# Two attention layers with two feed-forward layers: rows normalised by VectorE, and scores on four 64 by 64 tiles of TensorE with a softmax by even and odd heads

## What is computed

```
x = x + attention0(layernorm(x), ctx)      # 16 heads of 64, q = x@Wq, k = ctx@Wk, v = ctx@Wv
x = x + ffn0(layernorm(x))                 # silu(x@Wg) * (x@Wu), hidden 768, then @Wd
x = x + attention1(layernorm(x), ctx)      # a second set of weights
x = x + ffn1(layernorm(x))                 # rows and weights rounded to int8, product, scaled back

attention: scores = q @ k.T * 64**-0.5     # per head: 256 x 77
           attn   = softmax(scores)        # over the 77 keys
           out    = (attn @ v) @ Wo + bo
```

## Time and profile before

| | |
|---|---|
| median of 3 runs | 1615.76 us (1608.71 to 1623.88) |
| the profiled execution, its span | 1612.4 us |
| PE matmuls busy | 1554.2 us (96%), 27282 matmuls |
| ScalarE busy | 1371.5 us (85%) |
| VectorE busy | 1364.5 us (85%) |
| GpSimd busy | 1273.3 us (79%) |
| granted TensorE clock over the span | 0.992 of 2.4 GHz |

### The profile page before, as it was taken

One profiled execution on the slowest core, in us unless ns is written; L12 is line 12 of the kernel. 1 busy time (PEld: TensorE's weight loads), 2 busy tenths in 40 slices (PEclk: granted clock), 3 DMA queues, 4 the chain that ended last, 5 costly groups with the idle time before them and its releaser, 6 DMA issues.

```text
span 1612.4 us, 74691 instructions
## 1 busy us (share of the span) xinstructions
PE 1554.2 (96%) x27282; PEld 1438.8 (89%) x27282; DVE 1364.5 (85%) x3522; ACT 1371.5 (85%) x5640; POOL 1273.3 (79%) x1893
## 2 busy tenths in 40 slices
PE   7989898999999999999999999999999999999996
PEld 4555578999999999999999999999999999999995
DVE  6767567888888888888888887888898988998886
ACT  6656588899899989998999988889999999999984
POOL 5100088899999898999998988788999999999984
PEclk9999999999999999999999999999999999999998
DMA  9997689887887777878778999899899899988996
GB/s 262 366 274 250 232 170 186 169 175 173 183 166 173 177 173 169 176 173 183 166 173 179 171 173 160 154 183 189 193 200 199 190 192 193 202 191 193 190 189 124
DMA packets 740024, 307.81 MB, mean 191 GB/s; under 512 B 629201, under 2 KB 725361, under 8 KB 737841
## 3 DMA queue, kind: packets, MB, share of 16 engines
q1 hardware_dynamic: 738049, 299.32, 85.0%
q0 software_dynamic: 1840, 6.82, 1.4%
HBM read 87.09 MB, written 65.54 MB: 95 GB/s over the span
## 4 chain that ended last, share of the span: by engine, by line
PE 33%; POOL 32%; issue 11%; DVE 6%; DMA 3%; ACT 2%; SPq 1%; POOLq 0%; ACTq 0%; DVEq 0%
PE psum L328 25%; POOL pr L1660 10%; POOL p L1665 8%; POOL p L1673 6%; PE psum L1225 4%; POOL rs L388 3%; POOL hT_l L1651 3%; PE psum L326 2%; DMA pT<-p 2%; DVE oT_l L357 1%; PE psum L319 1%; DVE x L1640 1%; POOL y L1702 1%; ACT ex L1371 1%; DMA x2T<-x 1%
## 5 line engine op out<-in xcount | busy, mean ns | idle before, releaser
L1371 ACT ACTIVATE ex<-psum,nmax 128x77 f32<-128x77 f32 x2048 | 638.3, 336 | 43.2 <-DVE nmax L1499 35.9
L1665 POOL TENSOR_TENSOR p<-pr,p 128x308 f16<-128x308 f32 x512 | 414.2, 809 | 39.9 <-ACT p L343 1.8
L1371 ACT ACTIVATION_READ_ACCUMULATOR ex<-psum,nmax 128x1 f32 x2048 | 444.7, 217 | 0.0
L1660 POOL TENSOR_TENSOR pr<-ex,rden 128x308 f32<-128x308 f32 x512 | 375.0, 732 | 55.2 <-DVE rden L1504 54.5
L328 PE MATMUL psum<-xT,wq_h 128*64 128x256 f16 x4064 | 349.0, 273 | 0.0
L1499 DVE TENSOR_REDUCE nmax<-psum 128x4 f32<-128x308 f32 x512 | 240.7, 470 | 57.7 <-PE psum L328 55.8
L328 PE MATMUL psum<-xT,wq_l 128*64 128x256 f16 x2032 | 284.5, 273 | 0.0
L1673 POOL CAST p<-pr 128x308 f16<-128x308 f32 x509 | 242.2, 476 | 43.9 <-DMA pT<-p 12.0
L328 PE MATMUL psum<-kb,qT_h 128*64 128x154 f16 x4096 | 262.0, 231 | 8.7 <-PEq L398 4.6
L328 PE MATMUL psum<-wo_h,oT_h 128*64 128x256 f16 x1792 | 251.8, 275 | 11.7 <-DVE oT_l L357 10.2
L328 PE MATMUL psum<-wo_l,oT_h 128*64 128x256 f16 x1792 | 250.5, 273 | 0.0
(11 more groups left out here) (164 smaller groups left out, 3490.8 us busy)
## 6 DMA issues: line engine op xcount, KB each, us to landing
keys<-ks SPq DMA_DIRECT2D x16, 1232.0 KB, 7.7
kb<-keys SPq DMA_DIRECT2D x256, 77.0 KB, 2.8
vb<-vals SPq DMA_DIRECT2D x128, 154.0 KB
vals<-vs SPq DMA_DIRECT2D x64, 256.0 KB, 4.0
x_pair<-in_x_dram SPq DMA_DIRECT2D x32, 256.0 KB, 2.9
pT<-p SPq DMA_TRANSPOSE x512, 3.3
x_res<-in_x_dram SPq DMA_DIRECT2D x32, 256.0 KB, 3.1
mid_x<-y SPq DMA_DIRECT2D x32, 256.0 KB, 2.4
```

The lines of the kernel that those rows point to most:

```text
L1371: last = act.activation(ex[i][:, t, b, :], SC[:, t, b * NK:(b + 1) * NK], ACT.Exp, bias=nmax[i][:, t, b:b + 1], accum_out=den[i][:, t, b:b ...
L1660: pool.tensor_tensor(pr[:, t, :, :], ex[i][:, t, :, :], r, ALU.mult).then_inc(s_p, 1)
L1665: pool.tensor_tensor(d[:, t, 1, :, 0:NK], pr[:, t, :, :], d[:, t, 0, :, 0:NK], ALU.subtract).then_inc(s_pl, 1)
```

## The change

**Normalising.** `shift` and `nmr` go. `normalise` is now a step of VectorE: it waits for the inverse root, and makes two `tensor_scalar` instructions of 128 x 256, fp32 from SBUF to SBUF, each (x - mean) * inverse. ScalarE's steps go.

**Scores.** `scores` is called once in a unit, for both row halves. The array is cut into four tiles of 64 x 64: the 64 partitions of one head (`b` = 0 even, 1 odd) by the 64 rows of a quarter (`c`). A product has 77 columns of one head's keys. Results of even heads go to bank 0, of odd heads to bank 1. It waits for all exponentials of the unit before (`s_e` at `2 * k`). The second index of maxima, exponentials, reciprocals, probabilities and transposes now means the heads' parity, not the row half; their shapes stay, and so does their number. `weigh_values` reads the turned probabilities in that order.

**Order on VectorE.** `reciprocals` of the unit before (parity 1) stands before `maxima` of parity 0, and `maxima` of parity 1 directly behind `oT_l`, ahead of `normalise`.

```diff
-        def normalise(act, dst, src, rs, k, s_done):
+        def normalise(dve, k, dst, src, mv, rs, count, s_done):
+
+            dve.wait_ge(s_inv[k], count)
+            dve.sem_inc(s_stgo[k], 1)
             for t in range(QT):
-                act.activation(dst[:, t, :], src[:, t, :], ACT.Identity, scale=rs[:, t:t + 1],
-                               bias=nmr[k][:, t:t + 1]).then_inc(s_done, 1)
+                dve.tensor_scalar(dst[:, t, :], src[:, t, :], mv[:, t, 0:1], rs[:, t:t + 1], ALU.subtract,
+                                  ALU.mult).then_inc(s_done, 1)
...
-        def shift(dve, k, mv, rs, count):
-
-            dve.wait_ge(s_inv[k], count)
-            dve.scalar_tensor_tensor(out=nmr[k][:, :], in0=mv[:, :, 0], scalar=-1.0, in1=rs[:, :],
-                                     op0=ALU.mult, op1=ALU.mult).then_inc(s_nmr[k], 1)
...
-                def scores(k, u, t, k_need, halved):
-                    if t == 0:
-                        pe.wait_ge(s_ql, k + 1)
-                        pe.wait_ge(s_kb[u // 2], k_need)
-                    after(pe, s_e, QT * (k - 1) + t + 1)
+                def scores(k, u, k_need):
+
+                    pe.wait_ge(s_ql, k + 1)
+                    pe.wait_ge(s_kb[u // 2], k_need)
+                    after(pe, s_e, 2 * k)
+                    pe.sem_inc(s_sgo, 1)
                     i = u % 2
...
+                    terms = ((qT_h[i], 0), (qT_h[i], 1), (qT_l[i], 0))
+                    for t in range(QT):
+                        for a in range(PPU):
+                            at = slice((t * PPU + a) * NK, (t * PPU + a + 1) * NK)
+                            for q, (w, part) in enumerate(terms):
+                                done = (t, a, q) == (QT - 1, PPU - 1, len(terms) - 1)
+                                for b in range(2):
+                                    rows = slice(b * DH, (b + 1) * DH)
+                                    for c in range(2):
+                                        last = pe.matmul(SC[c * DH:(c + 1) * DH, b, at],
+                                                         w[rows, a, t * P + c * DH:t * P + (c + 1) * DH],
+                                                         kb[u // 2][rows, b, part, u % 2 * PPU + a, :],
+                                                         start=(q == 0), stop=(q == len(terms) - 1))
+                                    if done:
+                                        last.then_inc(s_s, 1)
...
-                        if lay[0] is not None:
-                            scores(n + u, u, 1, 0, True)
...
-                        if u == 0 and lay[-2] is not None and like <= NB:
-                            act.wait_ge(s_nmr[1], h - 1)
-                            if lay[-2] == 0 or like == B + 2:
-                                after(act, s_x216l, h - 2)
-                            normalise(act, x2, x1, rs2, 1, s_x2)
...
+                        if lay[(u - 1) // UNITS] is not None:
+                            reciprocals(n + u - 1, (u - 1) % 2, 1)
                         if lay[0] is not None:
                             maxima(n + u, u % 2, 0)
...
+                        if lay[0] is not None:
+                            maxima(n + u, u % 2, 1)
...
-                            shift(dve, 1, mv2, rs2, h - 1)
+                            normalise(dve, 1, x2, x1, mv2, rs2, h - 1, s_x2)
...
-                        if lay[0] is not None:
-                            maxima(n + u, u % 2, 1)
```

More of the change, by code:

```diff
@@ L280, in xattn_ffn_kernel @@
         s_inv = [sem(f"s_inv{i}") for i in range(3)]
-        s_nmr = [sem(f"s_nmr{i}") for i in range(3)]
         s_stgo = [sem(f"s_stgo{i}") for i in range(3)]
@@ L780, in _ @@
                         if (i, j) == (3, 33):
-                            shift(dve, 0, mv1, rs1, 1)
+                            dve.wait_ge(s_xt, 1)
+                            normalise(dve, 0, xn, x_in, mv1, rs1, 1, s_xn)
                         if (i, j) == (3, 37):
@@ L907, in xattn_ffn_kernel @@
         pr = sb("pr", [P, QT, HPU, NK], F32)
-        pT = [sb(f"pT_{i}", [P, 2 * HPU, NQ], F16) for i in range(UNITS)]
+        pT = [sb(f"pT_{i}", [P, 2, 2 * HPU, P], F16) for i in range(UNITS)]
         oT_h = [sb(f"oT_h{i}", [P, PPU, NQ], F16) for i in range(2)]
@@ L1183, in _ @@
             def _(pe):
-                def scores(k, u, t, k_need, halved):
-                    if t == 0:
-                        pe.wait_ge(s_ql, k + 1)
-                        pe.wait_ge(s_kb[u // 2], k_need)
-                    after(pe, s_e, QT * (k - 1) + t + 1)
-                    i = u % 2
-                    for a in range(PPU):
-                        o = SC[:, t, a * 2 * NK:(a + 1) * 2 * NK].rearrange("p (a k) -> p a k", k=NK)
-                        ts = slice(t * P, (t + 1) * P)
-                        for q, (w, part) in enumerate(((qT_h[i], 0), (qT_h[i], 1), (qT_l[i], 0))):
-                            last = product(pe, o, w[:, a, ts], kb[u // 2][:, :, part, u % 2 * PPU + a, :], halved,
-                                           start=(q == 0), stop=(q == 2))
-                    last.then_inc(s_s, 1)
+                def scores(k, u, k_need):
[3 more added lines that the diff above has]
+                    pe.sem_inc(s_sgo, 1)
+                    i = u % 2
+                    terms = ((qT_h[i], 0), (qT_h[i], 1), (qT_l[i], 0))
[13 more added lines that the diff above has]
+                                        last.then_inc(s_s, 1)
                 def project(k, u, l):
@@ L1224, in weigh_values @@
                                 c = (u % 2 * HPU + hd) * DH
-                                last = pe.matmul(o[b * DH:(b + 1) * DH, a, :], vb[u // 2][:, part, c:c + DH],
-                                                 pT[u][0:NK, pp * HPU + hd, :], start=(q == 0), stop=(q == 2))
+                                at = pp * HPU + a
+                                last = pe.matmul(o[b * DH:(b + 1) * DH, a, :].rearrange("p (t q) -> p t q", q=P),
+                                                 vb[u // 2][:, part, c:c + DH],
+                                                 pT[u][0:NK, b, at:at + PPU + 1:PPU, :], start=(q == 0), stop=(q == 2))
                     last.then_inc(s_pv, 1)
@@ L1546, in body @@
                         if u == 2 and lay[2] == 0:
-                            shift(dve, 0, mv1, rs1, h + 2)
+                            normalise(dve, 0, xn, x_in, mv1, rs1, h + 2, s_xn)
                         if lay[-1] is not None:
@@ L1563, in body @@
                         if u == 3 and lay[-3] == 0:
-                            shift(dve, 2, mv3, rs3, h - 2)
-                        if lay[(u - 1) // UNITS] is not None:
-                            reciprocals(n + u - 1, (u - 1) % 2, 1)
+                            dve.wait_ge(s_ys, 16 * (h - 2))
+                            normalise(dve, 2, yn, y, mv3, rs3, h - 2, s_yn)
                         if u == 1 and lay[-3] == 0:
```

23 lines of the change are left out of this document (7 added, 16 removed).

## The result

The changed kernel takes 1820.1 us (median of 4 runs, 1814.5 to 1822.0), the kernel before 1612.2 in the same session: the ratio is 1.129, 95% interval 1.124 to 1.134. The direction was the forecast's likeliest, but the forecast was 1641 us and its range ended at 1672. Its terms for the scores, the pair of rows and PE's own work came out close; two causes that it had costed at nothing, and the lock that came with the scores and that it had costed in two units alone, made the rest.

The account below looks back on a forecast made before the run. PE was taken to set the pace, three engines close behind. Bodies of 25.3 us (24.73 before) and 18.3 (18.09) add 18 and 7 us to 1612.4, giving 1637, or 1641 as median; range 1585 to 1672 for 8 in 10.

Parts of the forecast that it names:

- PE's own work: PE alone would need 24.05 us a body in layer 0 and 17.41 in layer 1, 0.68 less in each.
- the lock: Scores as a whole wait for the exponentials of half 1; costed in unit 0 of layer 0 and unit 1 of layer 1.
- Scores on PE: A unit's 48 products take 0.41 us plus 0.12 twice for the array's shape change: 0.65 in place of 0.82 us.
- Rival 3: Four tiles on PE don't run together: scores take 1.05 us a unit, about 1880 us in all; chance 7%.
- Its milder form: Half of the 269 us loss if one round of scores takes 0.051 us; most of that rival's 7%.
- The pair on VectorE: Two normalising instructions, taking turns with GpSimd, last 1.5 us until their end, between 0.9 and 1.9.
- Rival 1: The pair on VectorE is light, 0.9 us, as GpSimd doesn't get in between: about 1616 us; chance 23%.
- The sign of a second instruction that starts 0.7 us or more behind the first: Would show the forecast right: rows of L348 on VectorE, median over 0.5 us, the second 0.7 us or more behind.
- The load that the forecast made of the pairs: Three pairs add 3.1 us to VectorE in a body of layer 0, from 22.07 to 25.2 us.
- The chain through unit 0: In layer 0, scores wait behind pair, high half and exponentials, 6.05 us against 4.9 of PE work: PE stands 1.15 us.
- The rest ... has the same counts and sizes: Reciprocals' order, transposing DMAs, key loads and value products' read pattern cost nothing, hidden by GpSimd's softmax lead and free DMA time.

Follow-up runs that it names:

- e5: Changed kernel with PE's loop over layer 1 at one body a pass, and hidden(0) ahead of out_rows(0) on VectorE in unit 2: 1673 us.
- e7: Kernel before with the new scores, maxima and reciprocals only, rows still normalised by ScalarE, PE's loop at one body a pass: 1721 us.
- e9: Kernel before with one stronger wait: PE's scores of half 0 wait for the exponentials of both halves of the unit before: 1701 us.
- e10: e7 with hidden(0) early on VectorE, and ScalarE's normalising pairs and high half of x2 behind the exponentials of half 1: 1723 us.
- e3: Kernel before with only the normalising moved to VectorE; scores, exponentials and PE's program as before: 1657 us.
- e6: e5 with ScalarE's high half of x2 behind the exponentials of half 1 in place of ahead: 1665 us.
- e1: Changed kernel with PE's loop over layer 1 taking one body a pass in place of two: 1727 us.
- e14: e6 with only the pair of x2 on VectorE, and layer 1's high half of the turned rows between the halves' exponentials: 1625 us.
- e17: e14 with oT_l ahead of the moments of x1 on VectorE in unit 0: 1659 us.

## Why the prediction was right in the terms that it had and wrong in its sum

**Scores on PE: right.** 48 products run from 802.13 to the next instruction at 802.68, 0.55 us: 12 rounds of 0.035 and 0.12 on leaving. I had 0.41 and 0.12; what entering costs can't be read, as PE mostly waits there. PE's own work in a body is 24.05 and 17.5 us; the forecast had 24.05 and 17.41. Rival 3 is out. (Its milder form was also worked out wrongly: a round of 0.051 us makes 12 x 0.051 + 0.24 = 0.85 us against 0.82, 8 us in all; half of 269 needs rounds of 0.09.)

**The pair on VectorE: right, with a spread.** About 1.88 us for xn, 1.33 for x2 and 0.99 for yn, forecast 1.5 for each (0.9 to 1.9). One instruction of L348 takes 401 ns at its fastest and 948 for yn, 1352 for x_pair at its slowest. Rival 1, a light pair, is wrong for the first two and nearly right for yn. The sign of a second instruction that starts 0.7 us or more behind the first didn't come: for xn it starts 0.54 us behind and ends 1.27 behind. The load that the forecast made of the pairs was too large: VectorE is busy 24.2 us of a body of layer 0, not 25.2, up by 2.2 and not 3.1.

**The chain through unit 0: right in place and size.** PE waits 0.97 us in unit 1 of layer 0, 1.15 forecast; 0.92 in unit 1 of layer 1, 0.9 forecast. That the size fits is partly luck: once the stand at `down(1)` is gone, the same wait is 1.47 us (e5). And I took the new pair for its cause. e7 shows 1.33 us there with ScalarE doing the rows, and e9 0.97 with no change but the lock: the cause is the lock, and any pair between the halves lengthens it, ScalarE's (1.09 us of work and 0.37 for the shift) no less than VectorE's; with ScalarE's behind both halves (e10) this wait is gone. I worked out the lock for one unit of each layer and not for the rest: 0.25 us ahead of another unit's scores is its small change. Layer 1's 0.36 us for oT_l (0.15 before) comes with the scores part (e7) and neither with the lock alone (e9) nor with the rows (e3); its cause stays open. e6 shows what moving the high half out of the chain is worth: 7 us.

**The failed step: "The rest ... has the same counts and sizes".** By this step everything outside the terms above was put at nothing. Two things were not the same, and the list in it names neither.
- *The order on VectorE.* I costed the moved maxima, the pair ahead of `hidden(0)` and the scores gone from between `down(0)` and `down(1)` each where it stands, and didn't ask who waits for what is queued behind. The pair is 1.88 - 0.26 = 1.62 us longer than the shift in its place (749.52), the maxima add 0.38 (839.83 to 840.21), and PE has 0.41 us less to do meanwhile: 2.41 us, and PE waits 2.32. Either part alone gives 0.81: the shorter pair of e3 1.16 - 0.26 = 0.90, the maxima and scores of e7 0.38 + 0.41 = 0.79. e5 puts it at 54 us, the stretches at the lower clock among them.
- *PE's program.* I counted columns and not instructions. Twice as many products of half the columns cost PE no time, but two bodies of layer 1 no longer fit where PE keeps its program. e1 puts this at 1820 - 1727 = 93 us, the largest single term. The Trainium skill, "Advanced Engine Details and Errata", ISA Cache, gives TensorE 128 KB in lines of 16 KB, 256 instructions each. The traces agree with the size: 9.4 packets of 16 KB a pass are 150 KB and are fetched every pass; scaled by 1428/1814 the pass of before would be 7.4 packets, 118 KB as an estimate, and isn't. The same list says "Only 2 cache lines!", and there the traces differ: passes of 1001 and 1428 rows (before) run without a packet, and the measurement decides. At which size between 1428 and 1814 rows fetching sets in, no run shows.

**The sum.** From the changed kernel down: 1820, less 93 (program) is 1727, less 54 (bank) 1673, less 7 (unit 0) 1665, less 4 (turned rows) 1662, less 27 (two of three pairs back to ScalarE) 1634, less 10 is 1625; the 7 and the 4 are hardly clear of noise. The last 13 us over the kernel before are waits: in e14 PE stands 0.48 us for exponentials and 0.25 for oT_l in a body of layer 0, 0.31 and 0.36 in one of layer 1, where only the last was there before, at 0.15. PE's own load isn't among them, at 17.5 us a body of layer 1 in e14 against 17.94 before. What each of these waits costs I did not measure. The order in which causes are taken away decides their shares, since they cover one another: the rows part alone costs 45 us and the scores part in single passes 108, the two together 115.

**Where the expected gain went.** The four tiles save PE 0.6 us in a body of layer 0 (24.65 to 24.05) and 0.4 in one of layer 1 (17.94 to 17.53), 32 x 1.0 = 32 us; the forecast had 0.68 in both. All of it, and more, turns into waits, most of them for exponentials.

## What to carry to other kernels

Count instructions as well as columns: where a change splits an operation, compare the instructions in one pass of each engine's loop, and look in the DMA queues of the changed kernel for packets of kind instruction inside a loop. Where one operation replaces two that alternated over two buffers, ask what ran while the other half was in use; that overlap is lost even when the work shrinks. For each instruction that is moved or lengthened on an in-order engine, list what stands behind it and which bank, buffer or engine that sets free, since with four engines within 10% of the bound a shift of half a microsecond can cost 2% (e17).

## What the runs showed of the hardware

- Fetching the program again costs more than the wait for it, since the clock falls too. In the long body of layer 1 PE stands 3.9 and 2.1 us, and its busy time grows from 17.5 to 21.3 us at clock 0.50. In all a pass is 93 / 12 = 7.8 us longer, and this one 47.2 - 2 x 18.88 = 9.4.
- The clock falls to 1.2 GHz after a stand of 2.3 us in layer 0, but only in about every fifth body, though the same stand is in each: 3.4 us at 0.50 and 1.9 us lost. In the bodies of e7, with stands of 1.33 and 0.81 us, it never falls. After one such stand of the changed kernel, which ended at 531.26, PE worked 1.1 us more at full clock before it fell:

```profile
531.30:532.40 1.10, 1.10 (x22) 1.10 (x24) 0.51 (x1) 0.95 (x7) 0.49 (x1) 1.00 1.09 206
532.40:535.80 3.40, 3.40 (x38) 2.95 (x34) 1.76 (x6) 1.09 (x3) 1.90 (x3) 0.50 0.65 158
```

- Straight-line code fetched once doesn't hurt in the same way: in the kernel before the queue carries its 70 packets outside the two loops (up to 311 us, from 886 to 1114 and from 1520 on), and PE's largest wait for "issue" is 4.6 us, once.
- Four 64-by-64 tiles do run side by side: 0.035 us a round of four products of 77 columns, where a round of two with 154 columns took 0.068. The 48 products of one unit stand between 802.13 and 802.68 above.
